# First image of a ViT kernel on one core: the embedding's norm ahead of the first splits of the q/k weights, and the loads reordered

## The chip, the cores and the metric

One core of one Trainium2 chip runs the whole program. The metric is device time in microseconds, lower is better. Five engines work side by side: TensorE (PE, with its weight loads shown as PEld), VectorE (DVE), ScalarE (ACT), GpSimd (POOL) and SyncE (SP), which only issues DMAs here. They wait for each other by semaphores that the kernel sets by hand.

## The reference, cut to what matters

Input: 64 images of 224 x 224 x 3. Output: 64 x 197 x 192 in fp32. In order:

```
p = patches(x)                                  # (64, 196, 768)
h = layernorm(layernorm(p; ln1) @ W + b; ln2)   # embedding, D = 192, then a class token in front
h = h + attn(layernorm(h))                      # 12 heads of 64; q and k divided by the square root
                                                # of their norm over the heads, softmax(q k / scale[h]) v
h = h + ffn(layernorm(h))                       # 8 gated low-rank experts, top 2 of a softmax, added to a
                                                # second qkv projection; attention with 12 heads of 16
```

The first layer norm is not computed on the patches. With e = ln1_g * W, the product x @ e, the column sums of e and ln1_b @ W give the same result after the product: `(x @ e - mean * colsum(e)) * rstd + (b + ln1_b @ W)`.

## The kernel before, in words

Images are worked on one at a time, two per pass (s = 0 and 1), with the 197 tokens in two halves of 98 and 99 rows. `ORDER` is a list of steps written by hand; every engine goes through the same list and does its share of each step. Some steps belong to the image before (late stages) and some to the image ahead (marked `+`: X, EMB, LA, LB, LC), so the start of one image lies inside the attention of another. A pass called "start" does only the steps that are ahead, for the first image: nothing else is there to lie beside them.

The steps that matter here, for the first image:

- X: ACT squares the image, POOL adds the squares (L786, L501 to L503) into xss.
- EMB: PE multiplies the image with emb_w (L590), then, for the first image only, a row of ones with emb_w for the column sums (L595), then xss (L600). DVE makes the constants emb_cs (L916) and emb_b (L917) in `constants_of_embedding`, then mean, variance and the first part of the product (L1038 to L1045).
- LA: DVE scales and takes the statistics of the second norm (L1055, L1009, L1012). POOL turns a variance into 1 / sqrt (L519, L522), and DVE waits for it.
- LB: DVE applies that norm with tokc (L1063, L1068) and takes the statistics of the third.
- LC: DVE writes the normed tokens hn (L1018); then for the first image it runs `weights_of_scores` (L937 to L964), the second half of the splits of w_qk.
- T1: PE transposes hn (L563), ACT writes it in fp16 (L796), DVE writes the remainder (L1082). Only after it can PE begin q and k, L612.

A weight is "split" into an fp16 value times 64 and the fp16 remainder. `split_rows` (L923, L926) does this for the first 128 rows of w_qk, both halves of that on all 1536 columns; `split_packed` (L937, L940) does the last 64 rows. In the kernel before, `split_rows(qk_w, qk_raw)` stands at the head of DVE's "start" pass (L1025 to L1027), behind a wait for all loads of the group qk_loads, and thus ahead of everything DVE does for the first image except the product emb_w (L907).

The loads are all issued by SP, in the order emb_loads, image 0, norm_loads, qk_loads, v_loads, image 1, the rest (L447 to L455). Each group has one semaphore, and whoever waits for a group waits for all of it. DVE waits for norm_loads in `constants_of_embedding` (L914), PE ahead of T1 (`ident` is a part of mats_sb). POOL reads rowc in L508, behind hn_ready, with no wait of its own for the loads. Raw weights lie in buffers that are free at the start, and the trace shows them under those names: w_emb, ln1_bias, tok_bias in qk_sq, w_qk in vx, w_v in ebufs.

Of the kernel before, what the change touches and what calls it, by code (L numbers as in the profile page):

```python
# [153 lines left out]
def vit_tower(nc, x_t, w_emb, ln1, ln1_bias, tok_const, tok_bias, w_qk, w_v, w_out, w_gl, w_qkv2, w_lora_b,  # L154
# [4 lines left out]
    with ctx:  # L159
        def sb(name, shape, dt=F32):  # L160
            return ctx.enter_context(nc.sbuf_tensor(name, shape, dt))
# [4 lines left out]
        def sem(name):  # L166
            return ctx.enter_context(nc.semaphore(name))
# [3 lines left out]
        ln1_sb = sb("ln1_sb", [128, KC])  # L171
        tokc = sb("tokc", [TR, 2, 2, D])
# [5 lines left out]
        qk_w = sb("qk_w", [128, 3, 2 * INNER], F16)  # L178
# [9 lines left out]
        rowc = sb("rowc", [TR, 2 * D + NE + NE * RANK])  # L188
        mats_sb = sb("mats_sb", [128, 261])
# [80 lines left out]
        def flat(t, rows, first, *shape):  # L270
            n = int(np.prod(shape))
            names = "abc"[:len(shape)]
            return t[0:rows].rearrange("p a t -> p (a t)")[:, first:first + n].rearrange(
                f"p ({' '.join(names)}) -> p {' '.join(names)}", **dict(zip(names, shape)))

        emb_raw = flat(qk_sq, 128, 0, KC, D)
        ln1b_raw = flat(qk_sq, 128, KC * D, KC, TR)
        tok_b = flat(qk_sq, TR, KC * (D + TR) + H, 1, D)
        sel_raw = flat(qk_sq, 128, KC * (D + TR), H, 1)
        qk_raw = vx_both[:].rearrange("p s a h d -> p (s a h d)").rearrange("p (c f) -> p c f", c=2)  # L280
# [54 lines left out]
        emb_loaded, norm_loaded = sem("emb_loaded"), sem("norm_loaded")  # L335
        qk_loaded, v_loaded = sem("qk_loaded"), sem("v_loaded")
# [5 lines left out]
        def wait(eng, now, sig, p, earlier=None, by=1):  # L342


            n = now.count(steps[sig[0]], p, earlier)
            if n is not None:
                eng.wait_ge(sig[1], n * by)
# [13 lines left out]
        def passes(eng, body):  # L361
            body(Pass("start", -1))
            body(Pass("first", 0))
            for it in range(1, ITERS - 1):
                body(Pass("middle", it))
            body(Pass("final", ITERS - 1))
            body(Pass("last", ITERS))


        emb_loads = [(emb_raw, w_emb), (ln1_sb, ln1), (ln1b_raw, ln1_bias)]  # L370
        norm_loads = [(tok_b, tok_bias), (mats_sb, mats), (tokc, tok_const), (rowc, row_const)]
        qk_loads = [(scale_sb, scale), (sel_raw[0:64], head_rows[64:128]), (sel_raw[64:128], head_rows[64:128])]
        v_loads, loads = [], [(lorab_raw, w_lora_b), (proj_w[:, 2:3, :], w_proj[:, 2:3, :])]
        for j in range(4):
# [48 lines left out]
        @block.sync  # L423
        def _(sp):
            def load_group(group, loaded):
                for dst, src in group:
                    sp.dma_start(dst[tuple(slice(None) for _ in src.shape)], src).then_inc(loaded, 16)

            def load(n, s):
                sp.dma_start(xb[s][:], x_t[bass.ds(n * 2 + s, 1)].rearrange("b p c t -> (b p) c t")  # L430
                             ).then_inc(x_loaded[s], 16)

            def body(now):
                for kind, s, i in now.steps():
                    if kind == "QK" and i == 0 and now.which in ("first", "middle"):

                        wait(sp, now, pe_sig["EMB"], ("EMB", s, 0))
                        wait(sp, now, xsq_ready, ("X", s, 0))
                        load(now.it + 1, s)
                    elif kind == "OP2":  # L440
                        wait(sp, now, res_ready, ("OP2", s, 0))
                        dst = out[bass.ds(now.image((kind, s, i)) * 2 + s, 1)].rearrange("b t d -> (b t) d")
                        sp.dma_start(dst[1:1 + TO], res[s][0:TO, 0, :]).then_inc(stored[s], 16)
                        sp.dma_start(dst[1 + TO:NT], res[s][0:TO, 1, :]).then_inc(stored[s], 16)
                        sp.dma_start(dst[0:1], res[s][TO:TR, 1, :]).then_inc(stored[s], 16)

            load_group(emb_loads, emb_loaded)  # L447
            load(0, 0)
            load_group(norm_loads, norm_loaded)
            load_group(qk_loads, qk_loaded)  # L450
            load_group(v_loads, v_loaded)
            load(0, 1)
            load_group(loads, consts_loaded)
            sp.wait_ge(bias_cleared, 2)
            load_group(bias_loads, consts_loaded)  # L455
            passes(sp, body)
            for s in range(2):
                sp.wait_ge(stored[s], 48 * (ITERS + s))
# [438 lines left out]
        def _(dve):  # L897
# [13 lines left out]

            def constants_of_embedding():
                spare = next(b for b in range(8) if b not in [BANK[(k, s, 0)] for k in ("EMB", "T1") for s in range(2)])
                dve.wait_ge(norm_loaded, 16 * len(norm_loads))  # L914
                dve.wait_ge(setup_pe, 1)
                nc.vector.tensor_copy(emb_cs[:], psum[0:TR, spare, 0:D])  # L916
                nc.vector.tensor_tensor(emb_b[:], tok_b[:, 0, :], psum[0:TR, spare, D:2 * D], ALU.add  # L917
                                        ).then_inc(setup_dve, 1)
                dve.wait_ge(setup_dve, 2)

            def split_weights(dst, raw, by=WS):

                nc.vector.tensor_scalar(dst(0), raw, by, None, ALU.mult).then_inc(setup_w, 1)  # L923
                splits[0] += 1
                dve.wait_ge(setup_w, splits[0])
                return nc.vector.scalar_tensor_tensor(out=dst(1), in0=raw, scalar=by, in1=dst(0),  # L926
                                                      op0=ALU.mult, op1=ALU.subtract)
# [3 lines left out]
            def split_rows(w, raw):  # L931

                return split_weights(lambda v: w[:, v], raw[:, 0])
# [19 lines left out]
            def split_blocks(high, low, raw, by=WS):  # L953
                for (to_h, src), (to_l, _) in zip(head_blocks(high, raw), head_blocks(low, raw)):
                    split_weights(lambda v: (to_h, to_l)[v], src, by)
# [17 lines left out]
            def weights_of_attention2():  # L973
# [10 lines left out]
                for (to, src), (again, _) in zip(head_blocks(qkv2_w[:, 2], qkv2_raw[:, 1]),  # L984
                                                 head_blocks(qkv2_w[:, 3], qkv2_raw[:, 1])):
                    nc.vector.tensor_scalar(to, src, WS, None, ALU.mult)
                    nc.vector.tensor_scalar(again[0:64], src[0:64], WS, None, ALU.mult).then_inc(setup_w, 1)
                    splits[0] += 1
                    dve.wait_ge(setup_w, splits[0])
                    nc.vector.scalar_tensor_tensor(out=to[64:128], in0=src[64:128], scalar=WS, in1=to[64:128],  # L990
                                                   op0=ALU.mult, op1=ALU.subtract)
# [30 lines left out]
            def body(now):  # L1022
                dve.sem_clear(dve_chain)
                count[0] = 0
                if now.which == "start":  # L1025
                    dve.wait_ge(qk_loaded, 16 * len(qk_loads))
                    split_rows(qk_w, qk_raw)  # L1027
                for p in now.steps():
                    kind, s, i = p
                    done = rd_sig[kind][1] if kind in rd_sig else None  # L1030
                    b = BANK[p]
                    if kind == "EMB":
                        if s == 0 and now.image(p) == 0:
                            constants_of_embedding()
# [194 lines left out]
                    elif kind == "OP2":  # L1229
# [4 lines left out]
                                                ).then_inc(done, 1)  # L1234

            passes(dve, body)


# [65 lines left out]
```

## Time and profile before

| | |
|---|---|
| median of 3 runs | 3115.53 us (3112.74 to 3116.41) |
| the profiled execution | 3115.51 us, its span 3113.7 us |
| instructions | 98361 |
| PE, DVE, ACT, POOL busy | 95%, 75%, 63%, 19% of the span |
| mean granted clock of PE | 0.987 of full |
| DMA | 61.28 MB, mean 20 GB/s |

The span is what the profiler saw of the program; the time has 1.8 us around it. A time in the rows below is counted from the start of the span. A row of the timeline reads: start, duration, engine, line, operation, output <- inputs, shape, count, and in brackets how long the engine had been idle before and what released it.

### The profile page before, as it was taken

What the parts mean: (1) busy time and instruction counts of PE and PEld (TensorE: products, weight loads), DVE (VectorE), ACT (ScalarE), POOL (GpSimd) and SP (SyncE); (2) the same over time, 40 slices, a digit from 0 to 9 for tenths busy, and PEclk for the clock granted to TensorE, in tenths of its full rate; (3) what the DMA queues carried; (4) which work ended last, traced back from release to release, by engine and by line L of the source; (5) the groups of instructions that cost most, each with busy time, mean ns of one, the idle gap of its engine ahead of it and who ended that gap; (6) DMA issues with size and microseconds to landing.
All of it is one profiled execution on the core that took longest, in us unless ns stands there. A gap on an engine that the chain in (4) does not pass through costs nothing.

```text
span 3113.7 us, 98361 instructions
## 1 busy us (share of the span) xinstructions
PE 2965.3 (95%) x41624; PEld 2430.5 (78%) x41624; DVE 2328.8 (75%) x5441; ACT 1963.5 (63%) x3777; POOL 591.9 (19%) x859
## 2 busy tenths in 40 slices
PE   4899999999999999999999999999999999999996
PEld 4778877877877877877877888778778778778775
DVE  5777777777777777787777777777777777777773
ACT  2566666666666666666666666666666666666663
POOL 2111121121121121121121121121111111111210
PEclk7999999999999999999999999999999999999998
DMA  4000000000000000000000000000000000000000
GB/s 116 9 22 12 22 22 12 21 22 12 21 22 12 22 22 12 22 21 12 22 21 12 22 22 12 22 17 16 22 14 19 22 12 21 22 12 22 14 4 7
DMA packets 28389, 61.28 MB, mean 20 GB/s; under 512 B 4210, under 2 KB 18389, under 8 KB 27958
## 3 DMA queue, kind: packets, MB, share of 16 engines
q1 hardware_dynamic: 27958, 54.98, 6.1%
q8 instruction: 337, 5.52, 0.8%
q14 instruction: 94, 0.77, 0.1%
HBM read 45.29 MB, written 9.68 MB: 18 GB/s over the span
## 4 chain that ended last, share of the span: by engine, by line
PE 59%; DVE 35%; ACT 3%; issue 3%; DMA 0%; SPq 0%; POOL 0%; DVEq 0%; ACTq 0%
PE psum L686 9%; DVE mx L1118 8%; PE psum L695 8%; PE psum L590 8%; PE psum L612 7%; PE psum L622 4%; PE psum L722 4%; PE psum L674 3%; PE psum L656 3%; DVE st L1009 3%; DVE mx L1131 2%; PE psum L725 2%; DVE qk L1210 2%; PE psum L732 2%; DVE late L1227 2%
## 5 line engine op out<-in xcount | busy, mean ns | idle before, releaser
L850 ACT ACTIVATE ebufs<-psum 99x788 f32<-99x788 f32 x768 | 592.0, 823 | 58.1 <-PE psum L674 45.1
L519 POOL TENSOR_TENSOR veps<-mv,eps_ln 99x2 f32<-99x2 f32 x256 | 116.1, 453 | 2274.1 <-DVE mv L1040 1352.3
L1131 DVE TENSOR_REDUCE mx<-psum 99x4 f32<-99x788 f32 x384 | 357.5, 974 | 137.7 <-PE psum L639 137.4
L1118 DVE TENSOR_REDUCE mx<-psum 99x4 f32<-99x788 f32 x384 | 362.9, 974 | 52.1 <-PE psum L631 52.1
L612 PE MATMUL psum<-hn_s,qk_w 128*128 128x197 f16 x3840 | 354.9, 249 | 14.2 <-DVE hn_s L1082 7.2
L612 PEld LDWEIGHTS psum<-hn_s,qk_w 128*128 128x128 f16 x3840 | 323.0, 98 | 34.9 <-DVE qk L1210 19.0
L686 PE MATMUL psum<-ebufs,vx 98*32 98x197 f32 (+1 forms) x6144 | 293.6, 330 | 0.0
L695 PE MATMUL psum<-out_w,qk 128*99 128x192 f32 x1536 | 263.8, 329 | 0.1
L590 PE MATMUL psum<-emb_w,xb 128*99 128x193 f32 x1536 | 263.9, 327 | 0.0
L590 PEld LDWEIGHTS psum<-emb_w,xb 128*99 128x99 f32 x1536 | 249.1, 166 | 1.8 <-issue 1.4
L686 PEld LDWEIGHTS psum<-ebufs,vx 98*32 98x32 f32 (+1 forms) x6144 | 201.2, 110 | 57.5
L695 PEld LDWEIGHTS psum<-out_w,qk 128*99 128x99 f32 x1536 | 245.1, 166 | 0.3 <-issue 0.3
L622 PE MATMUL psum<-v_w,hn_s 128*99 128x384 f16 x1280 | 234.1, 330 | 0.0
L656 PE MATMUL psum<-qh,kh 64*99 64x197 f16 x1536 | 208.5, 255 | 17.5 <-DVE mx L1131 17.0
L1101 DVE TENSOR_TENSOR qk<-qk,ss 128x1182 f32<-128x1182 f32 x64 | 89.0, 1391 | 168.0 <-ACT ss L826 168.0
L802 ACT ACTIVATE qk_sq<-psum 128x788 f32<-128x788 f32 x192 | 158.8, 827 | 70.6 <-PE psum L612 70.6
L656 PE MATMUL psum<-ql,kh 64*99 64x197 f16 x1536 | 202.1, 246 | 0.0
L660 PE MATMUL psum<-neg_t,head_sel 64*99 64x197 f16 x1536 | 201.9, 246 | 0.0
L656 PE MATMUL psum<-qh,kl 64*99 64x197 f16 x1536 | 201.8, 245 | 0.0
L622 PEld LDWEIGHTS psum<-v_w,hn_s 128*99 128x99 f16 x1280 | 155.0, 127 | 47.1
L831 ACT CAST kh<-qk 128x1182 f16<-128x1182 f32 x64 | 75.6, 1181 | 176.4 <-DVE qk L1106 176.4
L1148 DVE TENSOR_TENSOR qk<-psum,rinv 128x394 f32<-128x394 f32 x192 | 108.9, 567 | 102.8 <-ACT rinv L861 62.1
(172 smaller groups left out, 6444.3 us busy)
## 6 DMA issues: line engine op xcount, KB each, us to landing
xb<-x_t SPq DMA_DIRECT2D x64, 591.0 KB, 3.9
out<-h SPq DMA_DIRECT2D x128, 73.5 KB
out<-h SPq DMA_DIRECT2D x64, 0.8 KB
vx<-w_qk SPq DMA_DIRECT2D x2, 384.0 KB, 11.2
qk_sq<-w_emb SPq DMA_DIRECT2D x1, 576.0 KB, 3.7
vx<-w_qk SPq DMA_DIRECT2D x1, 576.0 KB, 8.3
out_w<-w_out SPq DMA_DIRECT2D x8, 72.0 KB
late<-w_lora_b SPq DMA_DIRECT2D x1, 480.0 KB
```

Of the source, the lines that this page charges most:

```text
L590: nc.tensor.matmul(ps(p, slice(0, TR), slice(194 * t, 194 * t + D + 1)), xb[s][:, c, tile_cols(t)], emb_w[:, c, :], start=(c == 0), stop=( ...
L612: mm = nc.tensor.matmul(ps(p, slice(0, 128), slice(at, at + NT), m // 2), qk_w[:, w, f:f + 128], hn_s[s][:, v, c, 0:NT], start=(n == 0), s ...
L622: mm = nc.tensor.matmul(ps(p, slice(0, TR), slice(0, INNER // 2), b), hn_s[s][:, v, c, tile_cols(i)], v_w[:, w, INNER // 2 * b:INNER // 2 ...
L656: nc.tensor.matmul(ps(p, slice(0, TR), slice(NT * t, NT * t + NT), e), left[r], right[r], start=(n == 0), stop=False)
L660: mm = nc.tensor.matmul(ps(p, slice(0, TR), slice(NT * t, NT * t + NT), e), head_sel[r, 2 * i + e, :], neg_t[s][r, 0:NT], start=False, sto ...
L686: mm = nc.tensor.matmul(ps(p, slice(32 * j, 32 * j + 32), slice(NT * (c % 2), NT * (c % 2) + NT), c // 2), left, eb[0:n, j % 2, t, :], sta ...
L695: mm = nc.tensor.matmul(ps(p, slice(0, TR), slice(D * t, D * t + D)), o_t[s][:, m, tile_cols(t)], out_w[:, m, :], start=(m == 0), stop=(m ...
L722: nc.tensor.matmul(o, qkv2_w[:, w, f], hn2_s[s][:, v, c, 0:NT], start=(n == 0), stop=False)
L802: nc.scalar.activation(qk_sq[:, 4 * i:4 * i + 4, :].rearrange("p (b m) t -> p b (m t)", b=2), src, ACT.Square, scale=1 / WS)
L850: nc.scalar.activation(ebuf[n].rearrange("p e a t -> p e (a t)"), psum[0:TR, b + 2 * half:b + 2 * half + 2, 0:2 * NT], ACT.Exp).then_inc(r ...
L1118: nc.vector.tensor_reduce(mx[s][:, :, 2 * i:2 * i + 2].rearrange("p a e -> p e a"), psum[0:TR, b:b + 2, 0:2 * NT].rearrange("p e (a t) -> ...
L1131: nc.vector.tensor_reduce(mx2[s][:, :, at:at + 2].rearrange("p a e -> p e a"), psum[0:TR, b + 2 * half:b + 2 * half + 2, 0:2 * NT].rearran ...
```

## The change

On SP, the bias tok_bias goes from norm_loads to emb_loads, and the group qk_loads is issued before norm_loads, in which tok_const now comes first. On DVE the wait for norm_loads leaves `constants_of_embedding`; `split_rows(qk_w, qk_raw)` with its wait for qk_loads goes from the head of the pass to the step LB of the first image, behind EMB and LA, and the wait for norm_loads stands behind it. PE's waits, POOL and ACT have no edit.

```diff
-        emb_loads = [(emb_raw, w_emb), (ln1_sb, ln1), (ln1b_raw, ln1_bias)]
-        norm_loads = [(tok_b, tok_bias), (mats_sb, mats), (tokc, tok_const), (rowc, row_const)]
+        emb_loads = [(emb_raw, w_emb), (ln1_sb, ln1), (ln1b_raw, ln1_bias), (tok_b, tok_bias)]
+        norm_loads = [(tokc, tok_const), (mats_sb, mats), (rowc, row_const)]
...
             load_group(emb_loads, emb_loaded)
             load(0, 0)
+            load_group(qk_loads, qk_loaded)
             load_group(norm_loads, norm_loaded)
-            load_group(qk_loads, qk_loaded)
             load_group(v_loads, v_loaded)
...
             def constants_of_embedding():
...
-                dve.wait_ge(norm_loaded, 16 * len(norm_loads))
                 dve.wait_ge(setup_pe, 1)
...
-                if now.which == "start":
-                    dve.wait_ge(qk_loaded, 16 * len(qk_loads))
-                    split_rows(qk_w, qk_raw)
                 for p in now.steps():
...
+                    if kind == "LB" and s == 0 and now.image(p) == 0:
+
+                        dve.wait_ge(qk_loaded, 16 * len(qk_loads))
+                        split_rows(qk_w, qk_raw)
+                        dve.wait_ge(norm_loaded, 16 * len(norm_loads))
```

## Rows read from the trace of the kernel before

**Rows 1.** The page: busy time of PE, and the chain of waits by engine.

```profile
PE 2965.3 (95%) x41624; PEld 2430.5 (78%) x41624; DVE 2328.8 (75%) x5441; ACT 1963.5 (63%) x3777; POOL 591.9 (19%) x859
...
PE 59%; DVE 35%; ACT 3%; issue 3%; DMA 0%; SPq 0%; POOL 0%; DVEq 0%; ACTq 0%
```

**Rows 2.** Stretches of 50 us: length, PE busy, granted clock, DMA share, GB/s.

```profile
0.00:50.00 50.00, 18.78 (x116) 0.76 0.74 168
...
100.00:150.00 50.00, 44.73 (x511) 0.93 0.04 14
150.00:200.00 50.00, 48.88 (x697) 1.00 0.06 17
```

**Rows 3.** Timeline of DVE, from the first split of w_qk to LB.

```profile
19.87 0.96 DVE L923 TENSOR_SCALAR qk_w<-vx 128x1536 f16<-128x1536 f32 x1 [12.92 <-DMA vx<-w_qk]
...
22.54 0.35 DVE L916 COPY emb_cs<-psum 99x192 f32<-99x192 f32 x1
...
26.33 0.25 DVE L1012 BATCH_NORM_AGGREGATE mv<-st 99x2 f32<-99x6 f32 x2
27.66 0.75 DVE L1063 SCALAR_TENSOR_TENSOR h<-lnt,mv,tokc 99x192 f32<-99x192 f32 x2 [1.08 <-POOL rstd L522]
```

**Rows 4.** Timeline of PE, its first 47 us.

```profile
5.61 4.13 PE L534 MATMUL psum<-qk_sq 128*99 128x192 f32 x12 [5.61 <-DMA qk_sq<-ln_bias]
9.56 4.11 PE L590 MATMUL psum<-emb_w,xb 128*99 128x193 f32 x24
13.51 2.12 PE L595 MATMUL psum<-emb_w,xss 128*99 128x192 f32 x12
...
32.02 0.89 PE L563 MATMUL psum<-mats_sb,hn 98*128 98x98 f32 x4 [16.13 <-DVE hn L1018]
38.86 7.61 PE L612 MATMUL psum<-hn_s,qk_w 128*128 128x197 f16 x60 [5.95 <-DVE hn_s L1082]
```

**Rows 5.** Timeline of SP's queue: four of its entries.

```profile
1.67 0.43 SPq L427 DMA_DIRECT2D qk_sq<-ln_bias  x1
...
2.61 0.43 SPq L427 DMA_DIRECT2D qk_sq<-tok_bias  x1
...
8.43 2.40 SPq L427 DMA_DIRECT2D ebufs<-w_v  x4
...
10.88 0.58 SPq L430 DMA_DIRECT2D xb<-x_t  x1
```

**Rows 6.** DMA issues: the sizes of the three loads that are moved back.

```profile
tokc<-tok_const SPq DMA_DIRECT2D x1, 297.0 KB
...
rowc<-row_const SPq DMA_DIRECT2D x1, 201.1 KB
...
mats_sb<-mats SPq DMA_DIRECT2D x1, 130.5 KB
```

**Rows 7.** Tiles ebufs (w_v) and xb (three images): time to landing.

```profile
DMA to landing us min/median/max: 11.6/12.1/13.4
...
DMA to landing us min/median/max: 6.2/6.2/14.0
```

**Rows 8.** Timeline behind hn: DVE's last split and T1, ACT's square of image 1.

```profile
32.11 1.19 ACT L786 ACTIVATE qk_sq<-xb 128x1182 f32<-128x1182 f32 x1
...
32.78 3.82 DVE L940 SCALAR_TENSOR_TENSOR qk_w<-vx,qk_w 64x1536 f16<-64x1536 f32 x1
...
38.15 0.56 DVE L1082 TENSOR_TENSOR hn_s<-psum,hn_s 128x394 f16<-128x394 f32 x1
```

**Rows 9.** Stretches of 2 us: after the length PE, PEld, DVE, ACT, POOL, clock, DMA, GB/s.

```profile
18.00:20.00 2.00, 0.00 (x0) 0.00 (x0) 0.13 (x1) 0.00 (x0) 0.00 (x0) 0.95 1.00 201
...
38.00:40.00 2.00, 1.14 (x8) 1.08 (x9) 1.97 (x4) 0.00 (x0) 0.00 (x0) 0.50 0.16 47
...
42.00:44.00 2.00, 2.00 (x16) 1.85 (x15) 0.00 (x0) 1.65 (x5) 0.00 (x0) 0.57 0.00 0
```

**Rows 10.** Timeline of PE: the first two thirds of the same step for the second image.

```profile
80.26 3.58 PE L612 MATMUL psum<-hn_s,qk_w 128*128 128x197 f16 x40 [1.27 <-DVE hn_s L1082]
```

## The prediction

> **What bounds the kernel now.** I read the page first, then stretches of 50 us, then the timelines of each engine over the first 100 us. The page has PE busy 95% of the span, and the chain that ended last runs 59% over PE and 35% over DVE [rows 1]. The stretches show where the change can act at all: from 150 us on, PE is busy 48.88 of 50 us at full clock, pass after pass, while in the first 50 us it is busy for 18.78 us only [rows 2]. Of these passes the change alters nothing: it touches only the first image. So what it is worth is by how much the first passes move forward as a block, and its ceiling is the idle time at the start.
>
> There the order of waits is this. PE has done everything that the first image's embedding needs by 13.51 + 2.12 = 15.63 us [rows 4], and the constants and the norm on DVE could begin. But DVE stands until 19.87 us for the last load of w_qk, splits for 2.67 us, and only at 22.54 us begins with emb_cs [rows 3]. PE then waits 16.13 us for hn [rows 4]. From hn on, DVE works without a break (last splits, T1) up to 38.15 us, and releases PE's q and k at 38.86 us [rows 4, 8]. So from 19.87 to 38.7 us the end of the chain is DVE's list, and a us saved in it is one saved at L612.
>
> **The change part by part.**
>
> *One more load ahead of the start.* Both PE's first product (L534) and DVE's emb_w wait for the whole of emb_loads, and both began when ln1_bias landed, at 5.6 us, issued at 1.67 [rows 4, 5]. Now tok_bias belongs to the group. Its issue was at 2.61, behind image 0; it moves into image 0's place, 0.47 us behind ln1_bias, half of the 0.94 us between the two rows [rows 5]. Bounds: 0 (it is small and lands with ln1_bias) and 0.9 us (the whole distance). I take 0.4, near the spacing of one issue. PE has no gap between L534, L590 and L595: each group begins before the modelled end of the one ahead [rows 4]. So this is paid in full: column sums at 15.63 + 0.4 = 16.03 us. Image 0 is issued 0.47 us later too. Its landing 6.2 us behind an issue at about 2.14 was at 8.3 us, and L590 took it at 9.56 [rows 4, 7]: over a us of cover.
>
> *EMB and LA ahead of the split.* From the start of emb_cs, 22.54, to the end of LA's last statistic, 26.33 + 0.25 = 26.58, DVE needs 4.04 us [rows 3]. With 0.05 for the semaphore, DVE begins at 16.08 and is done at 20.12. Of the loads this stretch needs only tok_bias, for which DVE has already waited.
>
> *The split.* w_qk's last part landed at 19.87 us [rows 3]. Ahead of it 628.6 KB leave the queue [rows 6], which at the 201 GB/s of 18 to 20 us [rows 9] are 3.2 us; so it is there by about 16.7 us. Bounds: 15.5 us, if three issues of 0.4 us each [rows 5] came on top, and 19.9, if nothing is gained. All lie ahead of 20.12, so the wait for qk_loads costs nothing. The reordering of these loads buys nothing by itself: it only gives cover. The split itself costs the same 2.67 us and ends the stretch at 22.79.
>
> *What the split now hides.* LB waited 1.08 us for POOL's rstd [rows 3]. POOL now works beside the split, 2.67 us long; the wait goes. Its two small operations share nothing else with DVE's list.
>
> *The new wait for norm_loads.* Behind it on DVE stand LB, LC, the last splits and T1; PE's transposes and, through them, q and k wait for those. The three loads now lie in the queue where w_qk's end was, so they should land at about 19.9 us. Nearest rows on both sides: 16.7 (w_qk's own new landing) and the last of w_v, issued behind them, 13.4 us behind an issue at about 10.2 (the last of four from 8.43 to 10.83), so 23.6 us [rows 5, 7]. Against 22.79 the wait is 0 to 0.8 us. I take 0, as the loads of this queue landed in about the order of issue.
> The Trainium skill ("DMA: Bandwidth & Descriptors", Queues, rings and completion order) warns that completion is not first in, first out per issuing engine, since the 16 DMA engines finish independently. By that rule the end of the range, 0.8 us, would be the fairer figure; the landings here, 19.9, then 23.6, then 24.9 us in order of issue, do not ask for it.
>
> *Sum.* LB began at 27.66 and now begins at 22.79 + 0.03: 4.84 us earlier, made of 6.46 that EMB begins earlier (22.54 to 16.08, the 0.4 already off) plus 1.08 of hidden rstd, less 2.67 of split that is now inside, and less 0.03 of seam. From LB on the list is as before. L940 there took 3.82 us beside POOL [rows 8]; POOL's work is started by hn and by ACT's square of image 1, and moves with them. That square ran at 32.11 and now wants image 1 at 27.3; it landed 14.0 us behind its issue at 10.88, at 24.9 us [rows 5, 7, 8]: 2.4 us of cover, with the bytes ahead of it the same as before. w_v, at 23.6, is wanted at about 34. So L612 starts at 38.86 - 4.84 = 34.0 us, and unless the clock intervenes everything behind is 4.8 us earlier. 3115.51 - 4.8 = 3110.7 us; the profiled execution and the median, 3115.53, agree.
>
> **The clock of PE.** The granted clock was full until near 20 us, 4 us after PE fell idle, then 0.50 (1.2 GHz), and came back to 1.00 (2.4 GHz) within the stretch 42 to 44 us [rows 9], some 4.7 us into L612. PE still stands idle for about 11 us with the change, so it still falls. When it comes back is not mine to say: the 60 matmuls took 7.61 us, of the second image 40 took 3.58 at full clock, so 60 would take 5.37 [rows 4, 10]. From the best case (full at once) to the worst (half throughout, 10.74) the step moves by -2.2 to +3.1 us. I take 0, as most executions would lie between. There are more such stretches up to 150 us (clock 0.93 from 100 to 150 [rows 2]).
> The Trainium skill ("TensorE: Matmul & The Clock Gate", Part 1) says that the number of matmuls run at the low clock varies from run to run of one kernel with the phase at its start. By that rule the term has no fixed sign; one execution before can neither bear it out nor deny it.
>
> **The rivals.**
>
> 1. *The clock comes back sooner*, relative to the work, in L612 or in the stages behind it. For: the gap ahead shrinks by 5 us and the early stages lie close to the point of change. Against: nothing in the rows ties it to the gap's length. Price up to the 2.2 us above: 3115.5 - 4.8 - 2.2 = 3108.5 us. It is over the bound of 0.2% from 1.4 us on.
> 2. *The clock stays low longer*, and takes back part: +3.1 us at most in L612, so 3113.8. ACT, which must read the products anyway, hides some of it. Still no slower than before.
> 3. *Slower: the wait for norm_loads takes the place of the one removed.* DVE stands in front of LB, and hn is late. To be slower than before the loads must land after 27.66 us. If they came with the last bytes of the queue, which fade out in the stretch 38 to 40 us [rows 9], at 38.5, DVE would stand 15.7 us and the time would be 3110.7 + 15.7 = 3126.4 us. For: all groups stand in one long queue, busy without a gap at 18 us [rows 9]. Against: w_qk, issued in just that place, landed at 19.9, some 19 us ahead of the queue's last bytes.
> 4. *Nothing arrives at the end*, because a later step waits for something fixed in time. The only such things are loads, and all are done by 40 us, long before the second image's weights. Time 3115.5; I give it no more than a small share of rival 2.
>
> **How the numbers follow.** A measurement of this kernel can tell about 0.2%, 6.2 us, from no change. The forecast, 3110.7 (-0.16%), with 3108.9 to 3113.0 as its own range, has 0.57; rival 1 has 0.28; rivals 2 and 4 together 0.12; rival 3 0.03. Faster by over 0.2% is rival 1: 0.28. Within 0.2% are the forecast and rivals 2 and 4: 0.69. Slower: 0.03. The three runs before lie 3.7 us apart, which widens every case by some 1.5 us. The range for 8 in 10, from within rival 1 to the far end of rival 2, is 3106.5 to 3114.9.
>
> **What the changed profile would show.** PE's L534 begins at about 6.0 instead of 5.61 us. DVE's emb_cs begins near 16.1, with PE as the releaser; L923 near 20.1 with no idle time in front; LB near 22.8, with no wait for rstd or a DMA; PE's transposes near 27.2 instead of 32.02; L612 near 34.0. The second image's L612 at 80.26 comes 4.8 us earlier, give or take what the clock does, and the stretches after 150 us look as before. A wait for tokc, mats or rowc in front of L1063 would show rival 3; L612 at 34.0 with an end that is not 5 us earlier would show the clock or rival 4. I am wrong if L923 waits for w_qk again, if emb_loads land over 1 us later than before, or if the early stages swallow or double the shift.

## The result, and the profile after

| | before | changed |
|---|---|---|
| median of 22 runs each | 3115.55 us (3112.74 to 3118.08) | 3111.1 us (3109.35 to 3113.68) |
| the profiled execution, its span | 3115.51, 3113.7 us | 3109.35, 3107.6 us |

The ratio is 0.9986, with a 95% interval of 0.998 to 0.9992: 4.45 us less, where 4.8 were forecast. The profiled execution is the fastest of its 22; its span is 6.1 us shorter, about 1.6 us more than the medians lie apart, and the repeat below did not show that part again.

DVE's timeline of the changed kernel answers [rows 3] (columns as there):

```profile
6.02 1.36 DVE L907 TENSOR_TENSOR emb_w<-qk_sq,ln_sb 128x1152 f32<-128x1152 f32 x1 [6.02 <-DMA qk_sq<-tok_bias]
16.23 0.36 DVE L915 COPY emb_cs<-psum 99x192 f32<-99x192 f32 x1 [8.85 <-PE psum L595]
...
20.02 0.25 DVE L1011 BATCH_NORM_AGGREGATE mv<-st 99x2 f32<-99x6 f32 x2
20.19 0.93 DVE L922 TENSOR_SCALAR qk_w<-vx 128x1536 f16<-128x1536 f32 x1
21.15 1.76 DVE L925 SCALAR_TENSOR_TENSOR qk_w<-vx,qk_w 128x1536 f16<-128x1536 f32 x1
23.57 0.75 DVE L1064 SCALAR_TENSOR_TENSOR h<-lnt,mv,tokc 99x192 f32<-99x192 f32 x2 [0.66 <-POOL rstd L522]
...
34.07 0.56 DVE L1083 TENSOR_TENSOR hn_s<-psum,hn_s 128x394 f16<-128x394 f32 x1
```

DVE now waits for PE, not for w_qk. The split stands behind LA with no bracket, so nothing was waited for in front of it. But LB has one: 0.66 us for POOL's rstd, which the split was to hide. POOL's timeline in this stretch:

```profile
20.35 0.81 POOL L519 TENSOR_TENSOR veps<-mv,eps_ln 99x2 f32<-99x2 f32 x1 [1.87 <-DVE mv L1011]
21.24 2.22 POOL L522 TENSOR_TENSOR rstd<-veps,half_neg 99x2 f32<-99x2 f32 x1
...
26.39 0.69 POOL L522 TENSOR_TENSOR rstd<-veps,half_neg 99x2 f32<-99x2 f32 x1
```

The same operation on two columns took 2.22 us beside the split and 0.69 us alone. L519 ended at 21.16, with L922 (21.12); L522 ended at 23.46, 0.55 us behind the end of L925 (22.91).

PE's timeline answers [rows 4]; the last two rows are from where the second image's q and k are normed and the third image is embedded:

```profile
27.93 0.89 PE L563 MATMUL psum<-mats_sb,hn 98*128 98x98 f32 x4 [11.47 <-DVE hn L1017]
34.77 4.92 PE L612 MATMUL psum<-hn_s,qk_w 128*128 128x197 f16 x40 [5.96 <-DVE hn_s L1083]
40.16 1.88 PE L612 MATMUL psum<-hn_s,qk_w 128*128 128x197 f16 x20 [0.47 <-ACT qk L806]
...
90.24 0.90 PE L617 MATMUL psum<-ss,mats_sb 128*128 128x394 f32 x2 [2.39 <-DVE ss L1096]
90.98 4.10 PE L590 MATMUL psum<-emb_w,xb 128*99 128x193 f32 x24
```

PE's wait for hn fell from 16.13 to 11.47 us, and L612 starts at 34.77 instead of 38.86 us. By stretches of 50 us (columns as in [rows 2]), and PE's line on the page [rows 1]:

```profile
0.00:50.00 50.00, 21.70 (x125) 0.77 0.72 168
50.00:100.00 50.00, 38.45 (x432) 0.89 0.08 26
100.00:150.00 50.00, 44.18 (x568) 0.93 0.01 2
150.00:200.00 50.00, 48.54 (x705) 1.00 0.06 17
```

```profile
PE 2962.8 (95%) x41624; PEld 2428.5 (78%) x41624; DVE 2329.0 (75%) x5441; ACT 1963.4 (63%) x3777; POOL 594.1 (19%) x859
```

Past 150 us PE is as busy as before (48.54 against 48.88 of 50 us) and at full clock. How much earlier each mark came than in the kernel before, in two profiles of the changed kernel (the second is the repeat a0 told below), from the starts of the rows:

| mark | first profile | repeat |
|---|---|---|
| LB (L1063, now L1064) | 4.09 us | 3.98 us |
| L612, first image | 4.09 | 3.97 |
| sums of q and k (L1093, now L1094) | 4.44 | 3.60 |
| L612, second image | 5.04 | 3.48 |
| L1157, now L1158, of the first image | 5.99 | 3.36 |
| span | 6.1 | 3.3 |

### The profile page after: what moved, and what is told of

It is laid out like the page before. It is cut to its first block, busy times and chain, and to the rows that moved or that the text cites. A ratio compares the mean times of both kernels' runs of the same rounds, so it can differ in the third digit from the quotient of the medians.

```text
span 3107.6 us, 98361 instructions
## 1 busy us (share of the span) xinstructions
PE 2962.8 (95%) x41624; PEld 2428.5 (78%) x41624; DVE 2329.0 (75%) x5441; ACT 1963.4 (63%) x3777; POOL 594.1 (19%) x859
## 4 chain that ended last, share of the span: by engine, by line
PE 59%; DVE 35%; ACT 3%; issue 3%; POOL 0%; DMA 0%; SPq 0%; DVEq 0%; ACTq 0%
PE psum L686 9%; DVE mx L1119 8%; PE psum L695 8%; PE psum L590 8%; PE psum L612 7%; PE psum L674 4%; PE psum L722 4%; PE psum L622 4%; DVE st L1008 3%; PE psum L656 3%; DVE mx L1132 2%; PE psum L725 2%; DVE qk L1211 2%; PE psum L732 2%; PE psum L617 2%
## 5 line engine op out<-in xcount | busy, mean ns | idle before, releaser
L519 POOL TENSOR_TENSOR veps<-mv,eps_ln 99x2 f32<-99x2 f32 x256 | 116.7, 456 | 2266.5 <-DVE mv L1041 1344.9
L612 PE MATMUL psum<-hn_s,qk_w 128*128 128x197 f16 x3840 | 354.1, 249 | 14.9 <-DVE hn_s L1083 7.4
L612 PEld LDWEIGHTS psum<-hn_s,qk_w 128*128 128x128 f16 x3840 | 322.2, 97 | 35.6 <-DVE qk L1211 19.0
L590 PE MATMUL psum<-emb_w,xb 128*99 128x193 f32 x1536 | 264.0, 327 | 0.0
L590 PEld LDWEIGHTS psum<-emb_w,xb 128*99 128x99 f32 x1536 | 249.1, 166 | 1.4 <-issue 0.9
L656 PE MATMUL psum<-qh,kh 64*99 64x197 f16 x1536 | 207.9, 255 | 17.9 <-DVE mx L1132 17.0
```

Source lines behind the costliest of these rows:

```text
L590: nc.tensor.matmul(ps(p, slice(0, TR), slice(194 * t, 194 * t + D + 1)), xb[s][:, c, tile_cols(t)], emb_w[:, c, :], start=(c == 0), stop=( ...
L612: mm = nc.tensor.matmul(ps(p, slice(0, 128), slice(at, at + NT), m // 2), qk_w[:, w, f:f + 128], hn_s[s][:, v, c, 0:NT], start=(n == 0), s ...
L656: nc.tensor.matmul(ps(p, slice(0, TR), slice(NT * t, NT * t + NT), e), left[r], right[r], start=(n == 0), stop=False)
```

## The experiments

Each was timed beside the kernel before on its own chip, and groups a, b and c ran on three different chips. There are 11 executions of each, but 7 of b2, 6 of b3 and 5 of c1. Differences are those of the medians.

| kernel | median | before beside it | difference | ratio, 95% interval |
|---|---|---|---|---|
| a0 the change again | 3111.16 | 3115.47 | -4.3 | 0.9984 (0.9975 to 0.9993) |
| a1 DVE's order alone | 3110.59 | 3115.47 | -4.9 | 0.9984 (0.9975 to 0.9993) |
| a2 the loads alone | 3112.55 | 3115.47 | -2.9 | 0.9989 (0.998 to 0.9998) |
| a3 rstd ahead of the split | 3111.78 | 3115.47 | -3.7 | 0.9985 (0.9976 to 0.9994) |
| b1 first split in idle time | 3110.15 | 3116.65 | -6.5 | 0.9979 (0.997 to 0.9987) |
| b2 both splits ahead of EMB | 3108.42 | 3116.65 | -8.2 | 0.9972 (0.9961 to 0.9983) |
| b3 as b2, PE kept busy | 3106.29 | 3116.65 | -10.4 | 0.9969 (0.9957 to 0.998) |
| b4 the change, PE kept busy | 3109.75 | 3116.65 | -6.9 | 0.9979 (0.997 to 0.9988) |
| c0 the kernel before again | 3116.49 | 3116.05 | +0.4 | 1.0001 (0.9993 to 1.001) |
| c1 second split behind LA, PE kept busy | 3105.47 | 3116.05 | -10.6 | 0.9967 (0.9955 to 0.998) |
| c2 the loads alone again | 3112.76 | 3116.05 | -3.3 | 0.9988 (0.9978 to 0.9997) |
| c3 tok_bias on its own | 3110.52 | 3116.05 | -5.5 | 0.9983 (0.9975 to 0.9992) |

The intervals are some 3 us to each side, so neighbours in this table are told apart by their profiles, not by their times; c0 puts 0.4 us between two series of one program. Between the groups the kernel before itself differs by up to 1.2 us. So a gain over the changed kernel (a0) is given two ways where it matters: by the differences, and by the medians as they stand.

**a0 and c0: the same programs again.** No edit.

> The changed kernel once more, beside its variants on one chip. Theory: 4.1 us of the shift are DVE's list (LB at 23.6 instead of 27.7 us), the rest is where the clock of PE happens to return. Then LB is at 23.5 to 23.7 us again, the two operations of POOL for LB's rstd take some 0.8 and 2.2 us again, and the median lies near 3111 us. Rival, that the shift past LB (6.1 us in the span of the first profile) belongs to the change: the span is 3107.6 again.

> The kernel before, against itself: no edit. It shows what two series of the same program differ by, and gives a second profile of before. Theory (the clock's return and the landing of the loads move an execution by 1 to 2 us and nothing else): LB within 0.5 us of 27.66, the second image's L612 between 79 and 82 us, the median within 1 us of before's. Rival (the first profile of before was a late one by luck, and part of the shift at LB with it): LB at 27 us or earlier.

Of a0, DVE at LB and PE:

```profile
23.68 0.74 DVE L1064 SCALAR_TENSOR_TENSOR h<-lnt,mv,tokc 99x192 f32<-99x192 f32 x2 [0.66 <-POOL rstd L522]
```

```profile
34.89 7.97 PE L612 MATMUL psum<-hn_s,qk_w 128*128 128x197 f16 x60 [5.96 <-DVE hn_s L1083]
...
91.67 1.64 PE L617 MATMUL psum<-ss,mats_sb 128*128 128x394 f32 x2 [2.26 <-DVE ss L1096]
93.09 5.08 PE L590 MATMUL psum<-emb_w,xb 128*99 128x193 f32 x24
```

LB is within 0.11 us of the first profile, yet the span is 2.8 us longer (3110.4 us). The rows say where: L612 took 7.97 us in one piece against 4.92 and 1.88 us, and L617 with L590 took 1.64 and 5.08 us against 0.90 and 4.10. The granted clock of 90 to 98 us was 0.79 here and 1.00 there. So against this profile of before DVE's list is shifted by 4.0 to 4.1 us in both, and what lies past it goes with where the clock returned. Of c0, the first split, LB and the second image's L612:

```profile
20.72 0.96 DVE L923 TENSOR_SCALAR qk_w<-vx 128x1536 f16<-128x1536 f32 x1 [13.51 <-DMA vx<-w_qk]
...
28.51 0.75 DVE L1063 SCALAR_TENSOR_TENSOR h<-lnt,mv,tokc 99x192 f32<-99x192 f32 x2 [1.08 <-POOL rstd L522]
```

```profile
81.07 3.58 PE L612 MATMUL psum<-hn_s,qk_w 128*128 128x197 f16 x40 [1.28 <-DVE hn_s L1082]
```

LB was 0.85 us later than in the first profile, more than I had expected, since w_qk landed at 20.72 instead of 19.87 us. Of the two profiles of before the first is the early one. Against c0, LB of the changed kernel comes 4.94 and 4.83 us earlier, so the shift of DVE's list is 4.0 to 4.9 us, by where w_qk landed in the execution of before that it is set against.

**a1 and a2 with c2: the order on DVE, and the order of the loads.** Neither is a bare half: both keep tok_bias in the first group and the wait for norm_loads at LB. What the new order of the loads gives with that wait left ahead of emb_cs was not run.

```diff
# a1: the changed kernel with
-            load_group(qk_loads, qk_loaded)
             load_group(norm_loads, norm_loaded)
+            load_group(qk_loads, qk_loaded)
# a2, c2: the changed kernel with
+                if now.which == "start":
+                    dve.wait_ge(qk_loaded, 16 * len(qk_loads))
+                    split_rows(qk_w, qk_raw)
...
                     if kind == "LB" and s == 0 and now.image(p) == 0:
-                        dve.wait_ge(qk_loaded, 16 * len(qk_loads))
-                        split_rows(qk_w, qk_raw)
                         dve.wait_ge(norm_loaded, 16 * len(norm_loads))
```

> The new order on DVE and tok_bias in the first group, but w_qk loaded behind the constants of the norms, as before. Theory (the order on DVE is what pays, the new order of the loads only gives cover): w_qk lands near 19.9 us, DVE comes for it at 20.2, so LB is at 23.5 to 23.9 us and the time is that of the changed kernel, near 3111 us. Rival (the earlier w_qk pays): DVE stands for w_qk over 1 us and LB is past 24.7 us.

> The new order of the loads, but the split at the head of DVE's list as before; the wait for the norms' constants stays at LB. Theory: the two halves of the change are substitutes. w_qk lands at 15 to 15.5 us, the split runs to about 17.9, EMB starts then instead of at 16.2, LB comes 4.04 + 1.08 later, at 23.0 to 23.6 us, no later than in the changed kernel, and POOL's rstd takes 0.7 us again. Time near 3111 us. Rival (the order on DVE is needed): the split ahead of EMB costs its 2.67 us, LB at 26 us, time near 3113.5 us.

> The new order of the loads with the split at the head of DVE's list, once more, as its median was 1.4 us above the changed kernel's though LB came as early. Theory (that was chance in where the clock returns): its distance to the kernel before is now that of the changed kernel, 4.0 to 4.8 us. Rival (this order waits for a landing that varies, and the changed one does not): again about 3 us, and w_qk lands later than at 15.8 us in its profile.

DVE, then PE, of a1:

```profile
21.97 0.93 DVE L922 TENSOR_SCALAR qk_w<-vx 128x1536 f16<-128x1536 f32 x1
...
25.35 0.74 DVE L1064 SCALAR_TENSOR_TENSOR h<-lnt,mv,tokc 99x192 f32<-99x192 f32 x2 [0.66 <-POOL rstd L522]
```

```profile
7.03 4.16 PE L534 MATMUL psum<-qk_sq 128*99 128x192 f32 x12 [7.03 <-DMA qk_sq<-tok_bias]
10.98 5.04 PE L590 MATMUL psum<-emb_w,xb 128*99 128x193 f32 x24
15.86 2.12 PE L595 MATMUL psum<-emb_w,xss 128*99 128x192 f32 x12
```

With the old order of the loads DVE still waits for nothing in front of the split, and the time is the changed kernel's: the order on DVE is enough. This one profile does not bear out the forecast of LB (25.35 instead of 23.5 to 23.9), but for a reason upstream of both halves: the first group landed at 7.03 us, and PE reached L595 at 15.86, against 6.04 and 14.08. L922 could therefore not have shown a wait for a w_qk that landed at 20 to 21 us; that the cover holds when EMB is early rests on the time alone. Of a2, then of c2:

```profile
15.76 0.96 DVE L922 TENSOR_SCALAR qk_w<-vx 128x1536 f16<-128x1536 f32 x1 [8.41 <-DMA vx<-w_qk]
...
18.43 0.35 DVE L915 COPY emb_cs<-psum 99x192 f32<-99x192 f32 x1
...
23.61 0.74 DVE L1064 SCALAR_TENSOR_TENSOR h<-lnt,mv,tokc 99x192 f32<-99x192 f32 x2 [1.15 <-POOL rstd L522]
```

```profile
16.81 0.96 DVE L922 TENSOR_SCALAR qk_w<-vx 128x1536 f16<-128x1536 f32 x1 [9.30 <-DMA vx<-w_qk]
```

With the split left at the head of DVE's list the earlier loads bring w_qk to 15.8 to 16.8 us, 4 us ahead of before, and pay most of the gain: -2.9 and -3.3 us. The two edits are substitutes, not parts of a sum: 2.9 and 4.9 do not make 4.4. In a2 LB comes as early as in the changed kernel, in c2 at 24.67 us, a us later, with the landing: that speaks for the rival of c2, a stage that starts when w_qk lands. The step between -3.1 and -4.4 is too small for the runs to prove it.

**a3: rstd first, then the split.**

```diff
+                        wait(dve, now, rstd_ready, ("LA", s, 0))
                         dve.wait_ge(qk_loaded, 16 * len(qk_loads))
                         split_rows(qk_w, qk_raw)
```

> The changed kernel, with a wait for LB's rstd in front of the split, so that POOL and the split don't run at once. Theory (DVE's split holds POOL off SBUF): POOL's two operations take 0.2 and 0.7 us instead of 0.8 and 2.2, L922 starts 1.1 us later, LB is at 24.0 us, 0.4 us later than in the changed kernel, for no overlap at all is worse than a slow one. Rival (POOL was slow for another reason, the DMA queues for one): its operations stay at 0.8 and 2.2 us, and LB comes at 26 us. Time near 3111.5 us, not to be told from the changed kernel's.

POOL and DVE of a3:

```profile
21.80 0.19 POOL L519 TENSOR_TENSOR veps<-mv,eps_ln 99x2 f32<-99x2 f32 x1 [1.87 <-DVE mv L1011]
22.07 0.69 POOL L522 TENSOR_TENSOR rstd<-veps,half_neg 99x2 f32<-99x2 f32 x1
```

```profile
22.80 0.96 DVE L922 TENSOR_SCALAR qk_w<-vx 128x1536 f16<-128x1536 f32 x1 [1.08 <-POOL rstd L522]
...
25.47 0.74 DVE L1065 SCALAR_TENSOR_TENSOR h<-lnt,mv,tokc 99x192 f32<-99x192 f32 x2
```

With the split out of the way POOL took 0.19 and 0.69 us again, so it was the split that slowed it. LB is at 25.47 and not at 24.0 us because emb_cs came late here; compare the stretch between the two. From emb_cs (17.68) to LB are 7.79 us here, 7.34 in the changed kernel (16.23 to 23.57): 0.45 us worse, as expected. An overlap in which POOL is held off is still better than none; it hides 0.42 of 1.08 us.

**b1: the first split into DVE's idle time.** The first two loads of w_qk, with the three small ones ahead of them, get a semaphore; the split stands at the head of the pass, behind it, and only the wait for the rest of qk_loads stays at LB.

```diff
+        rows_loads, qk_loads = qk_loads[:5], qk_loads[5:]
...
+                if now.which == "start":
+                    dve.wait_ge(rows_loaded, 16 * len(rows_loads))
+                    split_rows(qk_w, qk_raw)
```

> The changed kernel, but the split of w_qk's first 128 rows goes into DVE's idle time in front of EMB, behind a semaphore of its own for the two loads it needs (and the small ones ahead of them). Theory (what counts is where DVE's 2.7 us of split lie, and DVE is idle from 7.4 to 16.2 us): the two loads land near 11.8 us, the split ends at 14.5, EMB begins at 16.2 as in the changed kernel, POOL's rstd for LB takes 0.7 us again and is waited for, LB is at 21.4 instead of 23.6 us, and the time falls by another 2.2 us to about 3109 us. Rival (the later stages give a shift this early back): 3111 us. Rival (the loads of w_qk land together, near 15 us): LB at 23 us and no gain.

```profile
13.92 0.96 DVE L925 TENSOR_SCALAR qk_w<-vx 128x1536 f16<-128x1536 f32 x1 [5.90 <-DMA vx<-w_qk]
...
16.80 0.36 DVE L918 COPY emb_cs<-psum 99x192 f32<-99x192 f32 x1
...
22.02 0.74 DVE L1068 SCALAR_TENSOR_TENSOR h<-lnt,mv,tokc 99x192 f32<-99x192 f32 x2 [1.18 <-POOL rstd L525]
```

The two loads landed at 13.9 us, 2 us later than I had thought. The same loads were there at 13.79, 12.97 and 12.02 us in b2, b3 and c1, so this is the late end. The split just fits: 1.66 us off LB against a0. The time is 6.5 us below before against 4.3, a gain of 2.2 us over a0 by the differences and 1.0 by the medians. By its own releaser LB at 22.02 us also shows that norm_loads had landed by then.

**b2: all work on w_qk ahead of EMB.** Three semaphores (scale and head rows; the first 128 rows; the rest). `weights_of_scores` does scale, head table, first split, second split at the head of the pass; the waits of DVE and ACT for emb_b count one more.

```diff
+                nc.vector.tensor_copy(head_sel[:], sel_raw.broadcast_to([128, H, TR]))
+                dve.wait_ge(rows_loaded, 16 * len(rows_loads))
+                split_rows(qk_w, qk_raw)
+                dve.wait_ge(qk_loaded, 16 * len(qk_loads))
+                split_packed(qk_w, qk_raw).then_inc(setup_dve, 1)
```

> The changed kernel, but all of DVE's work on w_qk, scale and the head table goes in front of EMB, with three semaphores for the loads in order of landing. Theory: the table and the scales run near 10 us, the first split at 12 to 14.5, the second from 15 to 17.9 us (about 2.9 us, as POOL is idle then, instead of 4.8), EMB begins at 17.9 (1.7 us later), LB is at 23.1, hn at 27.3, and T1's last step on DVE, which stood behind 6.4 us of splits, comes 2 us behind hn. L612 starts at 29.9 instead of 34.8 us; the time is about 3106.5 us. Rival (ACT's square of the second image, which comes between hn and T1's fp16 copy, or its load, becomes the wait): L612 at 31 to 32 us, time near 3108 us.

```profile
17.48 0.96 DVE L940 TENSOR_SCALAR qk_w<-vx 128x1536 f16<-128x1536 f32 x1 [0.76 <-DMA vx<-w_qk]
18.47 1.75 DVE L943 SCALAR_TENSOR_TENSOR qk_w<-vx,qk_w 64x1536 f16<-64x1536 f32 x1
20.26 0.36 DVE L919 COPY emb_cs<-psum 99x192 f32<-99x192 f32 x1
...
31.60 0.57 DVE L1086 TENSOR_TENSOR hn_s<-psum,hn_s 128x394 f16<-128x394 f32 x1 [1.83 <-ACT hn_s L800]
```

The last step of T1 comes 2.5 us behind hn instead of 7.0, and the second split takes 1.75 us where it took 3.8 beside POOL [rows 8]. But w_qk's last part landed at 17.4 us, so EMB began at 20.26 and not at 17.9, and L612 (32.31 us) not at 29.9. These 2.4 us at EMB are all that L612 is late by; ACT, the expected rival, is not needed for it, though the time, 3108.42 us, is the rival's. The gain over a0 is 3.9 us by the differences and 2.7 by the medians, where 4.6 were expected.

**b3 and b4: PE kept busy.** While PE waits for hn and for T1 it multiplies parts of emb_w into a bank that is free, 31 times on top of b2, 49 times on top of the changed kernel; the products are read by nobody. The first place in b4 (the second, 17 more in front of L612, looks the same; b3 has 26 and 5):

```diff
                         if kind == "T1":
+                            pe.wait_ge(setup_dve, 2)
+                            for n in range(32):
+                                nc.tensor.matmul(psum[0:TR, spare, 0:D], emb_w[:, 0, 0:TR], emb_w[:, 0, 0:D],
+                                                 start=True, stop=True)
                             pe.wait_ge(norm_loaded, 16 * len(norm_loads))
```

> As the one with all the work on w_qk in front of EMB, and PE multiplies 31 times into a bank that nobody reads while it waits for hn and for T1. Theory (the clock is the second price of the idle start): the granted clock stays at full from the start to L612, whose 60 matmuls take 5.4 to 5.6 us instead of 6.8 to 8; ACT reads the products and hides a part, so 1 to 2 us come off: about 3105 us. Rival (the clock costs nothing at the end, ACT and DVE bound that stage): no change in the time.

> The changed kernel and nothing else, but for 49 such multiplications of PE in its waits for hn and T1. Theory: L612's 60 matmuls take 5.4 to 5.6 us instead of 6.8 to 8.0, LB stays where it was, the time is 1 to 2 us below the changed kernel's, about 3109.5 us, and its executions lie closer together. Rival: no change in the time, 3111 us.

PE of b4 (the first row is its idle work in front of T1; the profile counts each of the fp32 products as two):

```profile
17.09 10.64 PE L577 MATMUL psum<-emb_w 128*99 128x192 f32 x64 [0.45 <-DVE emb_b L923]
...
34.99 3.58 PE L619 MATMUL psum<-hn_s,qk_w 128*128 128x197 f16 x40 [0.72 <-DVE hn_s L1090]
39.04 1.88 PE L619 MATMUL psum<-hn_s,qk_w 128*128 128x197 f16 x20 [0.48 <-ACT qk L813]
```

L612 (here L619) took 3.58 and 1.88 us, as the second image's does [rows 10], from a start at 34.99 us, where a0's started at 34.89. The stretch 34 to 42 us (columns as in [rows 2]), of b4, then of a0:

```profile
34.00:42.00 8.00, 5.73 (x62) 1.00 0.24 79
```

```profile
34.00:42.00 8.00, 7.11 (x52) 0.59 0.56 128
```

From the start of L612 to the sums of q and k are 7.55 us in b4, and 8.89 and 9.61 in the two profiles of the changed kernel; 8.14 in b3 and 9.14 in b2. So the clock's price in this stage is 1.0 to 2.1 us. The times agree: b4 gains 2.6 us over a0 by the differences and 1.4 by the medians, b3 gains 2.1 us over b2 beside it. That b4's runs lie closer together (2.5 us against a0's 3.7) shows nothing of the clock, as b1's, with no such products, span 2.3.

**c1: the best order found.** As b3, with 30 and 6 idle products, but the second split stands at LB, behind LA, and emb_b's waits are as in the changed kernel.

```diff
                     if kind == "LB" and s == 0 and now.image(p) == 0:
+                        dve.wait_ge(qk_loaded, 16 * len(qk_loads))
+                        split_packed(qk_w, qk_raw).then_inc(setup_dve, 1)
                         dve.wait_ge(norm_loaded, 16 * len(norm_loads))
```

> Scales, head table and the first split of w_qk in DVE's idle time in front of EMB; the second split behind LA, where it hides POOL's rstd; PE's 36 idle multiplications as in the two kernels with them. Theory: EMB begins at 16.8 us, the second split runs from 20.9 to 23.6 us, POOL is held off by it as by the first, LB is at 24.2 us, T1's last step on DVE at 30.2, L612 at 30.9 at full clock: as good as the version with both splits in front of EMB and the multiplications, or up to 1 us better, 10 to 11.5 us below the kernel before. Rival (w_qk's last two loads, which land near 16.5 to 17.5 us, are the true start of the stage): no gain over that version.

```profile
17.76 0.36 DVE L926 COPY emb_cs<-psum 99x192 f32<-99x192 f32 x1 [2.77 <-PE psum L606]
...
25.09 0.75 DVE L1076 SCALAR_TENSOR_TENSOR h<-lnt,mv,tokc 99x192 f32<-99x192 f32 x2 [0.66 <-POOL rstd L526]
```

DVE was done with the first split 2.77 us before PE had the column sums, so here the start of PE was the late one. The time, 3105.47 us, is 10.6 us below before (interval of the ratio 0.9955 to 0.998). Its slowest execution, 3106.41 us, is 2.9 us below the fastest of the changed kernel, though on another chip; against b3 it is the same.

**c3: tok_bias behind image 0, with its own semaphore.**

```diff
-        emb_loads = [(emb_raw, w_emb), (ln1_sb, ln1), (ln1b_raw, ln1_bias), (tok_b, tok_bias)]
+        emb_loads = [(emb_raw, w_emb), (ln1_sb, ln1), (ln1b_raw, ln1_bias)]
...
             load(0, 0)
+            load_group([(tok_b, tok_bias)], tok_loaded)
...
+                dve.wait_ge(tok_loaded, 16)
                 dve.wait_ge(setup_pe, 1)
```

> The changed kernel, but tok_bias is issued behind image 0 and has a semaphore of its own, so that PE and DVE begin as soon as ln1_bias has landed. Theory (its place in the first group costs the 0.4 us by which it lands later): L907 starts at 5.6 instead of 6.0 us or later, emb_cs at 15.8, LB at 23.2, and the time falls by 0.4 us, which the runs can't tell from none. Rival (the first group lands when it lands, whatever stands in it): L907 starts at 6.0 to 7.0 us as in the profiles so far.

```profile
5.44 1.36 DVE L909 TENSOR_TENSOR emb_w<-qk_sq,ln_sb 128x1152 f32<-128x1152 f32 x1 [5.44 <-DMA qk_sq<-ln_bias]
15.11 0.36 DVE L918 COPY emb_cs<-psum 99x192 f32<-99x192 f32 x1 [8.31 <-PE psum L597]
```

emb_w began at 5.44 us, emb_cs at 15.11 and LB at 22.46, 1.1 us ahead of the changed kernel. In the eleven profiles with tok_bias in the first group emb_w began at 5.92 to 7.01 us (median 6.66); in the three without it at 5.44, 5.59 and 5.85. The time, -5.5 us, agrees without proving it.

## Why the prediction was right, step by step

- **One more load ahead of the start: mis-sized.** I took 0.4 us and the first profile showed 0.43 (6.02 against 5.59). Over all profiles it is 1.1 us (medians 6.66 and 5.59), just past the far end of the bounds (0.9). "Paid in full" is not exact either: from L534's start to the end of L595 PE took 9.5 to 11.0 us over the fourteen profiles, so a0, whose products began 0.73 us later than the first profile's, had its column sums only 0.12 us later.
- **EMB and LA: right.** emb_cs at 16.23 against 16.08 us, then 4.04 us to the end of LA, to the hundredth.
- **The split and w_qk's landing: right.** Forecast near 16.7, bounds 15.5 to 19.9; measured 15.76 and 16.81 in a2 and c2, 16.39 and 17.48 in b3 and b2. "The reordering of these loads buys nothing by itself" was right of the changed kernel, as a1 shows, but wrong as a sentence: with the split left at the head of DVE's list it buys 3 us (a2, c2).
- **"POOL now works beside the split; the wait goes": failed.** 0.66 of the 1.08 us stayed. This is the step that failed. POOL's tiny operations each ended only when DVE's had; a3 took the split away and they were short again. The row of L940, 3.82 us beside POOL [rows 8], was in my hands and said that the two engines hold each other up.
- **The new wait for norm_loads: right.** It never showed as a releaser in front of LB, not even in b1, at 22.02 us.
- **The sum:** LB moved by 4.09 us in the profile and not by 4.84. The difference, 0.75, is the 0.66 us above and 0.15 us of a later emb_cs, less the seam of 0.03 and 0.03 us by which the stretch up to the split's end was shorter. That the time still lies 0.4 us from the forecast is in part luck: the forecast took w_qk to land at 19.87 us in the kernel before, and c0, at 20.72, shows that before can lose 0.85 us more, which is about what the rstd and the later emb_cs took away (0.81).
- **The clock: right to give it no sign.** By the spans the repeat gave back 0.7 us behind LB, the first profile gained 2.0. Rival 1 happened in that execution and not in the median. Its price, up to 2.2 us, was of the right size: 1.0 to 2.1 us in b3 and b4.
- **Rivals 3 and 4: no.** No load came late, and from 150 us on nothing was given back.

## What to carry to other kernels

In a start with idle time, list for each load when it lands and for each engine when it is free, and put work into the gap whose operand has landed, with a semaphore for just the loads it needs: b1 and b2 gained 2.2 and 3.9 us more that way than the change did (1.0 and 2.7 by the medians). Two edits that remove the same wait are substitutes; try each alone before adding their gains. Work put beside another engine to hide its latency hides only what the two do not share, and what a pause of PE costs must also be read in the stage behind it.

## What the runs showed of the hardware

DVE and POOL held each other up. POOL's operation on two columns took 2.22 instead of 0.69 us and ended 0.55 us behind DVE's operation with two inputs in SBUF, in six profiles alike (both of the changed kernel, a1, b4, c1 and c3); DVE's own split of 64 partitions took 3.83 us beside POOL's large sums and 1.75 without. The Trainium skill ("SBUF — State Buffer", SBUF: two separate sides) says of the SBUF ports that the two engines share that, where a DVE operation has two inputs in SBUF and GpSimd's reads SBUF too, whichever starts first holds them for its whole instruction and the other fully blocks. The trace agrees: L925 started first (21.15 against 21.24 us), and 0.55 us behind its end is nearly the operation's whole 0.69.

The column of the granted clock reads 1.00 from the start of the span, but PE's first product is slow: L534's 12 matmuls took 4.16 us where the 12 of L595, of the same shape, took 2.12. In a1 some six of L590's 24 must still have run at that pace (5.04 us instead of 4.10, at 0.17 us more for each; an estimate). Half the full clock would fit, as 4.16 is nearly twice 2.12, but no row shows it. Whatever the cause, where it ends differs from one execution to the next: from the start of L534 to the end of L595 are 9.5 us in c3 and 11.0 in a1.

What is left open: whether the loads alone are truly 1.3 us worse than the whole change, what they give without the moved wait for norm_loads, how much of the difference between the groups of runs is the chip, and by how much the landing of the first group varies with tok_bias out of it (three profiles).
